# Four-stage graph network on one core: a set waits for the gather group it names, and one block in eight of the last sum is made by one-hot products

## The reference, cut to what matters

```
h = _rel_graph_conv(features, src, dst, etypes, norm, comp1, V1, bias1)   # layer 1, twice
    H = jnp.einsum('ni,rio->nro', x, W)
    m = H[src, etypes] * norm
    agg = jax.ops.segment_sum(m, dst, num_segments=x.shape[0])
...
h = h + agg_edge                                                          # layer 3
neigh = jax.ops.segment_sum(h[src], dst, num_segments=N)
z = h + neigh
```

## Time and profile before

| | us |
|---|---|
| median of 3 runs | 7438.11 |
| lowest, highest | 7429.24, 7439.85 |
| span of the profiled execution | 5778.8 |
| POOL busy | 3969.2 (69%) |
| PE busy | 3412.2 (59%) |
| DVE busy | 2595.6 (45%) |
| ACT busy | 1457.5 (25%) |

### The profile page before, as it was taken

The page is one execution under the profiler, slowest core; times in us unless marked ns, Lnnn a source line. Parts: engine busy times, 40 slices in busy tenths (PEclk is TensorE's granted clock), DMA queues, the critical chain, the costliest instruction groups (busy, mean ns, idle before and its releaser), DMA issues. The chain is left out here.

```text
span 5778.8 us, 72791 instructions
## 1 busy us (share of the span) xinstructions
PE 3412.2 (59%) x18712; PEld 3084.7 (53%) x18712; DVE 2595.6 (45%) x8699; ACT 1457.5 (25%) x3506; POOL 3969.2 (69%) x4127
## 2 busy tenths in 40 slices
PE   3777777755433334777777776666676653333334
PEld 3676777634333333577777765566565543333333
DVE  4666656662222222433333356777777661111112
ACT  2222222210000000333333335665666410000002
POOL 6777777607777776577777727777777527777774
PEclk6555555576665565877777788999999875555556
DMA  4333333332222211422222226555666412222111
GB/s 126 107 105 109 108 107 107 82 121 87 62 63 64 61 53 49 139 60 60 60 60 60 60 78 168 160 158 158 159 159 159 109 38 53 53 53 53 53 53 41
DMA packets 392271, 522.01 MB, mean 90 GB/s; under 512 B 105994, under 2 KB 275937, under 8 KB 391513
## 3 DMA queue, kind: packets, MB, share of 16 engines
q0 software_dynamic: 131200, 271.80, 18.9%
q1 hardware_dynamic: 258009, 245.43, 14.0%
q10 hardware_dynamic: 2689, 0.36, 0.0%
HBM read 473.25 MB, written 50.76 MB: 91 GB/s over the span
## 5 line engine op out<-in xcount | busy, mean ns | idle before, releaser
L1047 PE MATMUL PS<-arena,att 128*128 x3328 | 735.4, 412 | 1219.5 <-DMA arena<-tab_h,HT 615.8
L1047 PEld LDWEIGHTS PS<-arena,att 128*128 128x128 f32 x3328 | 685.3, 315 | 1271.3 <-issue 1271.2
L1510 POOL DMA_INDIRECT arena<-tab_x,idx_a x880 | 831.4, 945 | 314.1 <-issue 265.5
L993 POOL DMA_INDIRECT arena<-tab_rel,idx_b x782 | 762.3, 975 | 397.3 <-issue 238.0
L679 POOL DMA_INDIRECT arena<-tab,idx_a x832 | 819.1, 984 | 259.4 <-issue 252.0
L993 POOL DMA_INDIRECT arena<-tab_h,HT x782 | 746.9, 955 | 300.5 <-issue 238.0
L491 POOL DMA_INDIRECT arena<-tab_rel,idx_b x782 | 741.0, 948 | 275.0 <-issue 238.0
L1024 DVE TENSOR_SCALAR att<-iota_row,drel 128x128 f32<-128x128 f32 x832 | 182.0, 307 | 814.5 <-PE PS L1047 814.4
L1020 DVE TENSOR_SCALAR att<-iota_row,drel,wgt 128x128 f32<-128x128 f32 x832 | 222.3, 364 | 694.3 <-PE PS L1047 694.2
L583 DVE TENSOR_TENSOR arena<-arena,PS 128x128 f32 x832 | 240.5, 289 | 598.8 <-PE PS L547 524.1
L543 PE MATMUL PS<-arena,att 128*128 x1664 | 368.3, 362 | 228.8 <-DMA arena<-tab_rel,idx_b 206.2
(11 more groups left out here) (374 smaller groups left out, 5252.6 us busy)
## 6 DMA issues: line engine op xcount, KB each, us to landing
arena<-pair_d SPq DMA_DIRECT2D x220, 256.0 KB
arena<-tab_u SPq DMA_DIRECT2D x880, 64.0 KB
arena<-drel_rows SPq DMA_DIRECT2D x104, 512.0 KB
tab_rel<-arena SPq DMA_DIRECT2D x50, 512.0 KB
arena<-tab_rel,idx_b POOLq DMA_INDIRECT x1564, 2.5
arena<-tab_x,idx_a POOLq DMA_INDIRECT x880
arena<-tab,idx_a POOLq DMA_INDIRECT x832
arena<-tab_h,HT POOLq DMA_INDIRECT x782
```

Of the source, the lines that this page charges most:

```text
L993: pool.indirect_dma_start(out=G[:, o:o + D], out_offset=None, in_=table, in_offset=bass.IndirectOffsetOnAxis(ap=src[:, c:c + 1], axis=0)). ...
L1047: ins = nc.tensor.matmul(acc, M[s % RM][:, k * P:(k + 1) * P], G[:, bass.ds(e * (2 * D) + g * D, D)], start=False, stop=True, skip_group_c ...
L1510: pool.indirect_dma_start(out=G[:, o:o + D], out_offset=None, in_=tab_x, in_offset=bass.IndirectOffsetOnAxis(ap=idx_pair[:, 4 * g + u:4 * ...
```

## The change

1. In all three ring sums PE waits for what it reads. DVE computes a row `need[s] = (estep[4s+3] >> 2) + 1`, the number of groups that set s needs (`needed_groups`). PE loads one number more per set (`load_need`) and waits for the semaphore `landed` to reach it. `landed` is counted up by POOL: after the third gather of group g POOL waits until group g-1 has landed and adds one; after the last gather it waits for the last group and adds one.
2. The last sum is a stage of its own, `stage_last_sum`. For the first 96 groups only 7 of the 8 blocks are gathered. The eighth is made on the chip, four groups ("a quad", QUADS = 24) at a time: SP loads the 512 source numbers broadcast to all partitions; DVE compares them with the node numbers of each of the 25 node tiles, which gives 25 selection matrices of 128x512 (ring of NS = 8); PE multiplies H by them and adds up in one PSUM bank (25 products with 512 columns, `pick`); ACT copies the bank to SBUF, PE turns it with four transposes (`turn`), ACT copies the result into place 7 of the four groups. The products of the next quad are spread over three of the four sets: 8, 8 and 9.

```diff
+        def needed_groups(dve, row, done):
+            dve.tensor_scalar(row, estep[:, 3::4], 2, None, ALU.arith_shift_right).then_inc(done, 1)
+            dve.wait_ge(done, 1)
+            dve.tensor_scalar(row, row, 1, None, ALU.add).then_inc(done, 1)
+
+        def load_need(eng, row, s):
+            return nc.values_load(row[0:1, s:s + 1], engines=[eng], min_val=1, max_val=GATHERS)
```

POOL's program, here of the first two ring sums:

```diff
                             ).then_inc(full[g % RG], 16)
+                            if g and c == 8 * g + 2:
+                                pool.wait_ge(full[(g - 1) % RG], 128 * ((g - 1) // RG + 1))
+                                pool.sem_inc(landed, 1)
+                    last = GROUPS_N - 1
+                    pool.wait_ge(full[last % RG], 128 * (last // RG) + 16 * (2 * ST - 8 * last))
+                    pool.sem_inc(landed, 1)
```

PE's program, in all three:

```diff
+                        groups = load_need(mybir.EngineType.PE, need, s)
                         pe.wait_ge(m_done, s + 1)
-                        if s < GROUPS_N:
-                            pe.wait_ge(full[s % RG], 128 * (s // RG) + 16 * min(8, 2 * ST - 8 * s))
+                        pe.wait_ge(landed, groups)
```

The new stage:

```diff
+        def stage_last_sum(name, table):
+            RG, RM, NS, GROUPS_N, QUADS = 16, 4, 8, -(-ST // 4), ST // 16
...
+            def gathers(g):
+                return 7 if g < 4 * QUADS else min(8, 2 * ST - 8 * g)
...
+            def chunks(s):
+                q, v = s // 4 + 1, s % 4
+                return [(q, c) for c in range(*((0, 8), (8, 16), (16, NT), (0, 0))[v])] if q < QUADS else []
...
+                @block.sync
+                        sp.dma_start(SRC[q % 2].rearrange("p (u e) -> p u e", u=4),
+                                     last_src[q, :, 3, P:2 * P].unsqueeze(0).to_broadcast([P, 4, P])
+                                     ).then_inc(s_src[q % 2], 16)
...
+                @block.scalar
+                    for q in range(QUADS):
+                        act.wait_ge(pick_done, NT * (q + 1))
+                        nc.scalar.copy(ROWS_T, BANK).then_inc(rows_done, 1)
+                        act.wait_ge(turn_done, q + 1)
+                        if 4 * q >= RG:
+                            act.wait_ge(sum_done, 4 * q + 3 - RG + 7)
+                        o = (4 * q % RG) * 1024
+                        nc.scalar.copy(G[:, o:o + 4096].rearrange("p (g k) -> p g k", g=4)[:, :, 7 * D:8 * D], v3(BANK)
+                                       ).then_inc(made, 1)
...
+                    def select(q, c):
...
+                        if i >= NS:
+                            dve.wait_ge(pick_done, i - NS + 1)
+                        dve.tensor_scalar(SEL[i % NS], SRC[q % 2], node[:, c:c + 1], None, ALU.is_equal
+                                          ).then_inc(sel_done, 1)
...
+                    def pick(q, c):
+                        i = NT * q + c
+                        pe.wait_ge(sel_done, i + 1)
+                        if c == 0 and q:
+                            pe.wait_ge(made, q)
+                        nc.tensor.matmul(BANK, H[:, c * D:(c + 1) * D], SEL[i % NS], start=(c == 0),
+                                         stop=(c == NT - 1)).then_inc(pick_done, 1)
...
-        stage_sum("s5", tab_h, False)
+        stage_last_sum("s5", tab_h)
```

More of the change, by code:

```diff
@@ L46 @@
 assert NB + TN - 1 <= PR and PR % 4 == 0
+GATHERS = -(-ST // 4)
 FAR, FLOOR = 2.0 ** 60, 2.0 ** 58
@@ L557, in _ @@
                     dve.sem_inc(s_ones, 1)
+                    needed_groups(dve, need, s_pos)
                     dve.tensor_scalar(pos, estep[:], 4 * RG - 1, None, ALU.bitwise_and).then_inc(s_pos, 1)
@@ L1029, in _ @@
                 def _(pe):
-                    parts = aside.tensor(pe) if aside else {}
+                    parts = aside.tensor(pe)
                     pe.wait_ge(s_zero, 1)
```

174 lines of the change are left out of this document (137 added, 37 removed).

## The result

The change takes 7408.94 us (median of 5 runs, 7404.61 to 7425.12), the kernel before 7438.11 (5 runs): a ratio of 0.9967, 95% interval 0.9954 to 0.9981. The forecast was 156 us, and 7408.94 lies outside its range. In what follows a cost in us beside a ratio is worked out from the ratio.

What follows compares the result with a forecast made beforehand. The prediction took POOL's gathers to set the length of all three ring sums. Its terms, -13.1 - 13.1 - 31 + 6 - 120.2 + 15 = -156 us, took 7438.1 to 7282 us, range 7245 to 7350 us (8 in 10).

Steps and rivals of the forecast that it cites:

- The median lies 1659 us above the span; I take that part as fixed: Whole program: time outside the profiled span stays, so the 156 us saved come straight off 7438.1 us.
- Rival E: Whole program: the part outside the span scales with program length, so 201 us saved, 7237 us; chance 0.04.
- The tails: Ends of the ring sums: fewer sets after the last landing; last -13.1, first -13.1, second -31 us.
- rival D: Second sum's tail stays, DVE's additions or edge-feature loads holding PE back; its 31 us fall away, 7313 us; chance 0.06.
- The notice: POOL's count-up of landed groups in the three ring sums: 0.02 us each, +6 us in all (0 to +88).
- POOL finds its wait fulfilled: Before POOL's count-up: the previous group has already landed, by a margin of 0.9 us, so POOL isn't held up.
- lies in its waits: PE's third load per set, 0.33 us, hidden in waits of 6 us per set (2.8 in the second sum).
- Rival C: POOL's count-up costs 0.30 us each, or the landing comes too late: +82 us, 7364 us; chance 0.08.
- The gathers: Last sum: POOL loses 96 gathers at 1.252 us each, -120.2 us.
- The comparisons: Last sum: DVE's 600 comparisons with 512 columns disturb POOL's gathers, +15 us (0 to 27).
- rival B: Last sum: comparisons lock POOL out for their whole 0.4 us, 240 us instead of 15, 7507 us; chance 0.04.
- Rival A: Last sum: PE becomes the bound because its clock isn't granted; 7340 us at 0.85, 7424 at 0.78; chance 0.10.

Runs made afterwards that it cites:

- c0: The kernel before, unedited, run for a new profile: 7472.84 us with a span of 7471.0 us.
- e13: The change with SP's edge-feature copy loop of the first ring sum shared with ACT: ratio 0.9865 to before, in a set without slow spells.
- e11: The change with the old waits and all but eight comparisons of the last sum one column wide: 5665.04 us, in a set without slow spells.
- e5: The kernel before, gathering 7 of 8 blocks in groups 16 to 95 of the last sum, nothing replacing the eighth: last sum 1034.4 us.
- e16: The change run again, word for word: ratio 0.9963 to the kernel before, with slow spells.
- e17: The kernel before with the change's new waits alone, in all three ring sums: ratio 1.0030, with slow spells.
- e15: The change with comparisons and one-hots in turn, SP's loop shared with ACT, loaded-number waits only from set 91: 7159.21 us, ratio 0.9629.
- e12: The change with the old waits, SP's loop shared with ACT, comparisons and one-hots in turn: ratio 0.9805, in a set without slow spells.

## Why the prediction was wrong

**The step that failed first** is "The median lies 1659 us above the span; I take that part as fixed". There is no such part: c0 has 1.8 us outside its span. What the timed executions have more is spells and pauses inside the five long stages, three of them those that the sum was about. There a gather of the last sum takes 1.43 us with the pauses instead of 1.252, and PE isn't close behind POOL. Rival E had doubted the step, in the wrong direction.

**The tails** (-13.1, -13.1, -31): with spells there is no gain. After the last gather PE has 203 rows left in the last sum and 687 in the second, against 112 and 329 in the trace shown, so it waits for its own backlog, not for a landing. In the first sum SP ends the stage. Without spells the second sum gave 27.6 us of its 29 (rival D falls), and e13 has 19 rows of PE left behind the last gather of the last sum, as forecast. But that sum's tail, from the start of the last gather to the end, went from 18.8 to 12.8 us only, and this step left something out: POOL's queue closes a stage with a drain of its own, here before and in e13,

```profile
L967 POOLq DRAIN  x2: 24076/24078/24079, 2270.7 to 5697.6; - x2
```

```profile
L1107 POOLq DRAIN  x1: 9196/9196/9196, 5646.2 to 5646.2; - x1
```

which was hidden by the seven sets in the trace shown (5697.6 to 5721.7, 10.0 us past the start of the last gather) and now begins behind the last count-up and ends at 5655.4, 12.6 us past it and 6.5 us after PE's last product. What was late next was POOL itself.

**The notice** (+6): the instruction costs 0.017 us as taken. But "POOL finds its wait fulfilled" was read from the end of one stage; in the first sum it fails, for 35 us without spells. The third load "lies in its waits" fails in the tails, 0.65 us for most of the sixteen sets. Rival C had the size of the cost wrong (82 us), but one of its two mechanisms is what the first sum shows: a landing that comes too late, not the price of the instruction.

**The gathers** (-120.2): right without spells (122.4 measured in e11). With them a gather is worth 1.43 us (e5).

**The comparisons** (+15): 44 us without spells. Two gathers of 1.07 and 1.13 us beside seven short operations were read as the whole price, and the upper bound, 27 us, came from another stage. What rival B says is seen where comparisons follow without a gap, but over all of them it comes to 44 / 600 = 0.07 us each; from 0.29 on it would have decided against the change. The Trainium skill (SBUF — State Buffer, "SBUF: two separate sides") states the exclusive lock of the port pair, held for the whole instruction, for a VectorE operation in a 2-port perf mode; whether these comparisons are such, no row shows. The 3.14 us gather agrees with such a lock; the whole sum of rival B does not come of it, since between most comparisons there is a gap in which the gather gets on.

**PE's side**: 0.91 granted in e13's last sum (4750 to 5640 us), 758.87 of 890 us busy, and PE isn't among what POOL waited for. Rival A falls where its terms hold; with spells PE is late, but not by its clock, which is 0.84 in the change's last sum and 0.57 in c0's.

Without spells the sum of the terms is about -82 us (e13: +30.2, -27.6, -84.1; timed -78), so even there half of the 156 would have been missing: 41 in the first sum (35 of POOL's late wait, the rest mostly of the tail that the drain keeps), 32 in the last (29 of the comparisons, 7 of that tail, less some 4 of small terms), 1 in the second. With spells the products give 49 us of the last sum and the waits take 19 to 22 us of the program. That the time fell at all, as forecast, rests on the gathers alone; the waits were forecast to give 51 us and gave nothing.

What stays open: what the 0.70 us are, why POOL's gathering brings them on for PE and SP, and whether it is the chip or its state at the time. Where they are, the longer gathers make 686 x (1.045 - 0.950) = 65 of the 88 us that the products cost, and the tail after the last gather another 15 (54.2 us in e16, 39.5 in e17); the other 8 are not accounted for. Whether comparisons in turn and late waits together reach the forecast without spells is open too.

## What to carry to other kernels

Before a sum is made on a trace, hold its span against the timed runs: a gap of a fifth was not overhead here but another kind of execution, in which the pacemaker's step had another price and the engine behind it another backlog. A wait put into the queue of the engine that sets the pace costs what its lead used to absorb; it belongs where the lead is no longer needed, near the end, though the one run with it there (e15) had spells and no tail to win. Work that is hidden beside a gathering POOL should leave it gaps: wide DVE operations one by one, with short ones between.

## What the runs showed of the hardware

- The same kernel took 5789 us in one set of runs and 7438 to 7474 in five others. The difference is in spells, while POOL gathers, in which PE's and SP's instructions start some 0.70 us apart or a multiple of it; POOL's gathers keep their 0.944 us, and the eight stages with no or few gathers keep their length (432 and 434 us in all).
- A spell isn't a wait for instructions from memory as far as the transfers show it: between 6330 and 6440 us of c0, 39 slow rows of PE, the queues carry the gathers and one block of instructions.

```profile
q0 software_dynamic: 2816, 5.77, 20.1%
q14 instruction: 1, 0.01, 0.0%
```

- A gather beside comparisons of 512 columns that follow each other without a gap lasted up to 4.0 us (0.944 alone); with a one-hot between any two, 1.43 us at most (e12).
- POOL's drain at the end of a ring sum ended 10.0 us past the start of the last gather in the kernel before (both traces); with a wait for the last landing ahead of it, it took 9.0 to 9.2 us and ended 12.3 to 12.6 us past that start (e13).
